# First causal attention: four heads of a group at once in three rounds instead of two heads in six, and the norms of a batch a group earlier

## The reference, cut to what matters

```python
attn = jnp.einsum('bhqd,bhkd->bhqk', q, k) * scale
attn0 = jnp.where(mask, 0.0, attn)
attn = conv_general_dilated(attn0, kernels, ...)   # 3x3 for each (batch, head)
attn = jnp.where(mask, -jnp.inf, attn)
p = jax.nn.softmax(attn, axis=-1)
out = jnp.einsum('bhqk,bhkd->bhqd', p, v)
return out @ proj_W + proj_b
```

## Time and profile before

| | us |
|---|---|
| three runs | 1775.22, 1777.56, 1786.68 |
| median | 1777.56 |
| the profiled execution | 1798.3, its span 1796.6 |
| of it the sixteen groups of the first attention (136.0 to 522.9) | 386.9 |

### The profile page before, as it was taken

The page is one execution under the profiler, slowest core; times in us unless marked ns, Lnnn a source line. Parts: engine busy times, 40 slices in busy tenths (PEclk is TensorE's granted clock), DMA queues, the critical chain, the costliest instruction groups (busy, mean ns, idle before and its releaser), DMA issues. The chain is left out here.

```text
span 1796.6 us, 26122 instructions
## 1 busy us (share of the span) xinstructions
PE 1290.6 (72%) x9324; PEld 773.9 (43%) x9324; DVE 1040.1 (58%) x2987; ACT 534.9 (30%) x1061; POOL 598.8 (33%) x744
## 2 busy tenths in 40 slices
PE   1378898998866893566454499789866988987820
PEld 0333344443434893465454388323325953332210
DVE  2455565565642344799999466435334435457797
ACT  0123343333322551222131133124313522323310
POOL 7032322224133253111032444101244531155675
PEclk9988997899987996555555599869857998867665
DMA  4900000000004121643351121310001220022232
GB/s 127 338 1 1 1 1 0 1 1 13 1 12 131 45 72 49 155 111 102 82 140 30 40 60 56 122 39 1 13 24 47 72 66 12 0 71 67 80 99 82
DMA packets 74246, 106.20 MB, mean 59 GB/s; under 512 B 11501, under 2 KB 55712, under 8 KB 71616
## 3 DMA queue, kind: packets, MB, share of 16 engines
q1 hardware_dynamic: 59968, 72.16, 14.3%
q0 software_dynamic: 14144, 32.32, 5.9%
HBM read 77.10 MB, written 27.33 MB: 58 GB/s over the span
## 5 line engine op out<-in xcount | busy, mean ns | idle before, releaser
L833 POOL DMA_INDIRECT y_d<-arena,goal x138 | 132.4, 960 | 185.8 <-DVE arena L916 112.0
L2032 POOL DMA_INDIRECT wide<-in_w_ud,arena x128 | 130.5, 1020 | 82.0 <-DVE arena L2063 45.1
L1701 DVE CUSTOM_DVE_ANT_0 arena<-ps,far 128x512 f32<-128x512 f32 (+3 forms) x256 | 117.8, 488 | 59.6 <-PE ps L1375 59.0
L2959 PE MATMUL ps<-wide,arena 78*128 78x32 bf16 x3840 | 110.1, 187 | 49.9 <-ACT wide L3072 41.5
L1290 POOL TENSOR_SCALAR_AFFINE_SELECT arena<-arena 128x260 f32<-128x260 f32 (+1 forms) x128 | 53.1, 427 | 255.8 <-ACT arena L1568 255.8
L2959 PEld LDWEIGHTS ps<-wide,arena 78*128 78x128 bf16 x3840 | 109.3, 104 | 56.2 <-ACT wide L3072 45.4
L1012 PEld LDWEIGHTS ps<-arena 128*128 128x128 f32 (+1 forms) x1012 | 123.2, 191 | 4.1
L1012 PE MATMUL ps<-arena 128*128 128x128 f32 (+1 forms) x1012 | 123.6, 274 | 0.0
L1568 ACT ACTIVATE arena<-ps 128x1024 f32<-128x1024 f32 (+1 forms) x96 | 84.6, 882 | 106.8 <-PE ps L1397 106.6
L1397 PE MATMUL ps<-arena 32*128 32x128 f32 (+3 forms) x512 | 112.2, 486 | 1.1 <-DVE arena L1720 1.1
L2583 DVE TENSOR_REDUCE arena<-ps 128x6 f32<-128x462 f32 (+1 forms) x96 | 55.2, 582 | 84.0 <-PE ps L2323 76.8
(11 more groups left out here) (514 smaller groups left out, 2637.7 us busy)
## 6 DMA issues: line engine op xcount, KB each, us to landing
arena<-low_d SPq DMA_DIRECT2D x32, 780.0 KB
xs_d<-zrow SPq DMA_DIRECT2D x1, 10320.0 KB, 35.6
arena<-xs_d SPq DMA_DIRECT2D x69, 129.0 KB, 2.1
arena<-y_d SPq DMA_DIRECT2D x16, 256.0 KB, 3.2
arena<-in_w SPq DMA_DIRECT2D x2, 1408.0 KB
y_d<-arena,goal POOLq DMA_INDIRECT x138
wide<-in_Wfc SPq DMA_DIRECT2D x1, 2048.0 KB, 11.5
wide<-in_Wproj SPq DMA_DIRECT2D x8, 256.0 KB, 6.2
```

The source lines that it names most:

```text
L833: pool.indirect_dma_start(out=y_d, in_=yb[:, i % 2, c, :], in_offset=None, out_offset=bass.IndirectOffsetOnAxis(ap=goal[:, i % 4, c:c + 1] ...
L1701: ins = nc.vector.tensor_tensor_reduce(junk[:, n % 2, 384 * i:384 * i + w], ps[:, n % 2, 384 * i:384 * i + w], far[:, T - w:T], 1.0, 3 * N ...
L2032: pool.indirect_dma_start(out=rows_g[t % 4][:, h, :], out_offset=None, in_=A["w_ud"], in_offset=bass.IndirectOffsetOnAxis(ap=eidi[:, t % 8 ...
L2959: mm = nc.tensor.matmul(ps[:, 2 * (i % 3) + h // 2, col:col + 4 * HD], ring[m_ % 4][:, h * NK + p_, t % 2 * P:t % 2 * P + P], table[n // 4 ...
```

## The change

Six rounds of two heads become three rounds of four heads, with the same key tiles in each round. The four heads' scores go to banks 2 to 5, one bank each, in every round, so the scores of a round wait for all exponentials of the round before. The exponentials stay 1024 wide: two instructions (two heads each) in the first and second round, one over four heads in the third. `pt` is one buffer for four heads, in which each round has its own columns. `select` works on four heads at once. The loops of TensorE and ScalarE are rewritten for three rounds; on GpSimd `products` now stands ahead of the last `select`, and `rstd0` with `near_weights` moves from groups 2 and 6 to groups 1 and 5. On VectorE `outputs(G-1)` moves from behind `maximum_out` to between the ninth and the tenth maximum, `norms` moves to the end of groups 0 and 4, and `normed` to the start of groups 2 and 6.

```diff
--- before.py
+++ after.py
@@ -1166,7 +1166,7 @@
         def first_causal():
             at[0] = 0
             q3 = carve(3, T); kpad = carve(2, T + 2); kc = carve(3, T)
-            pt = carve(2, 2, 1280); junk = carve(2, T)
+            pt = carve(4, 1280); junk = carve(2, T)
             xnp = carve(2, T + 3); xn0 = carve(NT, D)
             stat = carve(2, NT, 6); mean = carve(2, NT, 2); rst = carve(2, NT)
             nq = carve(7, D); prod = carve(9, D); near_dots = carve(9, H); near_two = carve(2, 9, H)
@@ -1247,6 +1247,7 @@
 
             mean_uses = [(r0 + r, ts) for r0 in (0, 2) for ts in ((3,), (2, 0), (1,)) for r in range(2)]
             ROUNDS = [((0, 0),), ((1, 0), (3, 384)), ((2, 0),)]
+            exps_after = lambda n: 5 * (n // 3) + (2, 4, 5)[n % 3]
             COL = {0: 0, 1: 512, 3: 896, 2: 1024}
 
             with nc.Block() as block:
@@ -1283,12 +1284,12 @@
                                                 pb0[:, :].unsqueeze(1).to_broadcast([P, NT, D]), ALU.add).then_inc(c["pb"], 1)
 
                     def select(n):
-                        pool.wait_ge(c["exp"], n + 1)
+                        pool.wait_ge(c["exp"], exps_after(n))
                         for kt, _ in ROUNDS[n % 3]:
                             w = min(T - P * kt, P + 2)
-                            v = pt[:, n // 3 % 2, :, COL[kt]:COL[kt] + w]
+                            v = pt[:, :, COL[kt]:COL[kt] + w]
                             ins = nc.gpsimd.affine_select(out=v, in_=v, compare_op=ALU.is_ge, fill=0.0, base=-2,
-                                                          pattern=[[0, 2], [1, w]], channel_multiplier=-1)
+                                                          pattern=[[0, 4], [1, w]], channel_multiplier=-1)
                         ins.then_inc(c["sel"], 1)
 
                     rstd0(0)
@@ -1303,21 +1304,19 @@
                     for G in range(G4):
                         nb, nt = near_key(G)
                         to_experts = lambda t: scatter(pool, 0, G // 4 - 2, rows0, twins0, t, t + 1) if G % 4 == 3 and G >= 11 else None
-                        for rd in range(3):
-                            select(6 * G + rd)
+                        select(3 * G)
                         to_experts(0)
-                        if G % 4 == 2 and G // 4 + 2 < B:
+                        if G % 4 == 1 and G // 4 + 2 < B:
                             rstd0(G // 4 + 2)
                             near_weights(G // 4 + 2)
-                        select(6 * G + 3)
+                        select(3 * G + 1)
                         to_experts(1)
                         if G % 4 == 2 and G >= 6:
                             R_.rstd_of(pool, ch, G // 4 - 1)
-                        select(6 * G + 4)
-                        to_experts(2)
                         if nb < B:
                             products(nb, nt)
-                        select(6 * G + 5)
+                        to_experts(2)
+                        select(3 * G + 2)
                         to_experts(3)
                         if G % 4 == 2 and G // 4 + 2 < B:
                             residual_bias(G // 4 + 2)
@@ -1384,30 +1383,28 @@
                         mm.then_inc(turn7, 1)
 
                     def scores(G, rd):
-                        n = 6 * G + rd
+                        n = 3 * G + rd
                         if rd == 0:
                             pe.wait_ge(free7_dve, emptied(place7["mz", G])[1])
                             pe.wait_ge(c["kc"], G + 1)
-                        if n >= 2:
-                            pe.wait_ge(c["exp"], n - 1)
-                        for kt, o in ROUNDS[rd % 3]:
-                            for i in range(2):
-                                r = rd // 3 * 2 + i
+                        if n:
+                            pe.wait_ge(c["exp"], exps_after(n - 1))
+                        for kt, o in ROUNDS[rd]:
+                            for r in range(4):
                                 rows = slice(32 * r, 32 * r + 32)
-                                mm = nc.tensor.matmul(ps[:, 2 + n % 2 * 2 + i, o:o + T - P * kt], kc[rows, G % 3, P * kt:P * kt + P],
+                                mm = nc.tensor.matmul(ps[:, 2 + r, o:o + T - P * kt], kc[rows, G % 3, P * kt:P * kt + P],
                                                  q3[rows, G % 3, P * kt:T], start=True, stop=True)
                         mm.then_inc(c["s"], 1)
 
                     def weighted(n):
-                        G, rd = n // 6, n % 6
+                        G, rd = n // 3, n % 3
                         pe.wait_ge(c["sel"], n + 1)
                         if rd == 0 and G:
                             pe.wait_ge(c["pvout"], G)
-                        for kt, _ in ROUNDS[rd % 3]:
-                            for i in range(2):
-                                r = rd // 3 * 2 + i
+                        for kt, _ in ROUNDS[rd]:
+                            for r in range(4):
                                 mm = nc.tensor.matmul(ps[32 * r:32 * r + HD + 1, 6, P * kt:T], v9[:, G // 4 % 3, kt, 4 * (G % 4) + r, :],
-                                                      pt[:, n // 3 % 2, i, COL[kt]:COL[kt] + T - P * kt], start=kt == 0, stop=kt == 2)
+                                                      pt[:, r, COL[kt]:COL[kt] + T - P * kt], start=kt == 0, stop=kt == 2)
                         mm.then_inc(c["pv"], 1)
 
                     def outputs_turned(G):
@@ -1454,40 +1451,34 @@
                         scores(G, 0)
                         top(2)
                         if G:
-                            weighted(6 * G - 1)
-
+                            weighted(3 * G - 1)
                         top(3)
-                        scores(G, 1)
-                        top(4)
                         if G + 2 <= last:
                             keys(G + 2)
+                        top(4)
                         top(5)
-                        weighted(6 * G)
+
+                        scores(G, 1)
                         if G % 4 == 1 and G >= 5:
                             joined(G // 4 - 1)
-
                         top(6)
-                        scores(G, 2)
-                        top(7)
                         if nb < B:
                             shifted(nb, nt, 0)
+                        top(7)
+                        weighted(3 * G)
                         top(8)
-                        weighted(6 * G + 1)
-
-                        top(9)
-                        scores(G, 3)
-                        top(10)
                         if G:
                             outputs_turned(G - 1)
-                        top(11)
-                        weighted(6 * G + 2)
+                        top(9)
+
+                        scores(G, 2)
                         if nb < B:
                             shifted(nb, nt, 1)
-
-                        scores(G, 4)
+                        top(10)
+                        weighted(3 * G + 1)
+                        top(11)
                         if nb < B:
                             shifted(nb, nt, 2)
-                        weighted(6 * G + 3)
                         if G % 4 == 1 and G >= 5:
                             projected(G // 4 - 1)
                         if G % 4 == 2 and G // 4 + 2 < B:
@@ -1498,12 +1489,9 @@
                             R_.logits(pe, take, G // 4 - 2)
                         if G % 4 == 2 and G >= 10:
                             R_.places(pe, take, G // 4 - 2)
-
-                        scores(G, 5)
-                        weighted(6 * G + 4)
                         if G + 1 <= last:
                             maximum_rows(G + 1)
-                    weighted(6 * last + 5)
+                    weighted(3 * last + 2)
                     outputs_turned(last)
                     R_.logits(pe, take, 2)
                     joined(B - 1)
@@ -1560,16 +1548,17 @@
                         ins.then_inc(free7_act, 1)
 
                     def exps(G, rd):
-                        n = 6 * G + rd
+                        n = 3 * G + rd
                         act.wait_ge(c["s"], n + 1)
-                        if n >= 6:
-                            act.wait_ge(c["pv"], 3 * (n // 3 - 2) + 3)
-                        o, w = ((0, 512), (512, 512), (1024, 256))[rd % 3]
-                        nc.scalar.activation(pt[:, n // 3 % 2, :, o:o + w], ps[:, 2 + n % 2 * 2:4 + n % 2 * 2, 0:w], ACT.Exp, scale=SCALE)\
-                            .then_inc(c["exp"], 1)
+                        if G:
+                            act.wait_ge(c["pv"], n - 2)
+                        o, w, heads = ((0, 512, 2), (512, 512, 2), (1024, 256, 4))[rd]
+                        for r in range(0, 4, heads):
+                            nc.scalar.activation(pt[:, r:r + heads, o:o + w], ps[:, 2 + r:2 + r + heads, 0:w], ACT.Exp, scale=SCALE)\
+                                .then_inc(c["exp"], 1)
 
```

(34 more changed lines are left out.)

## The result

The median went from 1782.12 us (four runs of the kernel before in the same session) to 1731.16 us (1724.08 to 1734.80). The ratio is 0.971, interval 0.965 to 0.977. The forecast was 1746, with a range of 1712 to 1787.

A forecast was written before the change was run, and what follows sets the result against it. TensorE was taken to set the pace, with VectorE in chains it waits for. The groups fall from 386.9 to 328.5 us at full clock, 58 gained, less 27 for the clock, rounded 32: 1777.6 - 32 = 1746 us, range 1712 to 1787.

The forecast's parts named there:

- The mechanism: TensorE, plain group: four heads cost what two do, saving 2.4 us on weighted values and 1.5 on scores; 20.54 to 16.6.
- The rival in which four column groups don't run side by side: Weighted values: 2.4 us x 16 = 39 us come back, giving 1785 us; chance 0.13.
- the one in which the clock falls twice a group: Pauses at the third maximum product and before `maximum_rows`: 28 falls cost 95 us against 58 gained, 1815 us; chance 0.08.
- the rival of the exponentials: One set of score banks makes TensorE wait in two rounds per group, a microsecond a group lost, 1762 us; chance 0.14.
- The rival in which the clock stays up: Pauses pull TensorE's clock down no more than once or twice; 58 us gained, 1720 us; chance 0.20.
- The clock term: Groups 1 to 10: pauses over 2 us make TensorE's clock fall eight times, 3.4 us each, 27 us lost.
- The sum at full clock: All sixteen groups at 2.4 GHz: 328.5 us against 386.9 before, 58 us gained; plain group 19.3 us.
- The chain from the last shifted product to the third maximum product: Groups 0 to 10: copy, `products`, `near_scores`, first maximum take 7.0 us; TensorE has 4.7 beside it, so 2.3 sticks out.
- the extras of groups 1 to 10: Norms and picks, join, `projected` with `maximum_rows`: 24 us on top of ten plain groups, 193 + 24 = 217.
- The join: VectorE, groups 4 and 8: 4.9 us, of which the chain covers 1.7, so 3.2 us in each.
- The moves: Earlier `outputs(G-1)` and moved norms remove waits of 0.92, 1.68 and 2.72 us, inside the 19.3; moved work costs 2.4 per batch.
- The exponentials: ScalarE ahead of the next round's scores: margin 0.6 us in groups 11 to 13, 1.9 in the others; no cost.

The follow-up runs named there:

- run with halves apart: Changed kernel with the weighted values issued two heads at a time again, a maximum product between the pairs: 1763.61 us, ratio 0.986.
- run with scores apart: Changed kernel with scores issued two heads at a time again in the first and third round: 1786.37 us, ratio 0.999.
- the late near scores: Changed kernel with `near_scores` of a group done in the next group, behind `mixed_keys`, six maxima later: 1785.18 us, ratio 1.002.
- the spread-out join: Changed kernel with the eight instructions of `join` between the maxima of groups 5, 9 and 13, its transposes later: 1743.98 us, ratio 0.978.
- four fills: Changed kernel with 22 products nobody reads ahead of the queries in groups 0, 5, 9 and 13: 1753.90 us, ratio 0.986.
- one maximum later: Changed kernel with `near_scores` of a group behind the first maximum of the next group instead of ahead of it: 1730.48 us, ratio 0.975.

## Why the prediction was right, and which terms were off

**The mechanism** was right in its main step: TensorE's work per plain group falls by 4 us (predicted 20.54 to 16.6, measured 16.55), of it 2.4 for the weighted values, which the run with halves apart confirms. The rival in which four column groups don't run side by side is refuted, and so is the one in which the clock falls twice a group: it lost 31 us in the stage, not 95. So is the rival of the exponentials: TensorE waits for them 1.1 us in all in front of L1395. The rival in which the clock stays up fails too, though its time, 1720, is nearer to the result than mine. The stage was to give 31 us (58 less 27) and gave 49.8. The terms, measured for each group as in the table above:

| | predicted | measured |
|---|---|---|
| groups 1 to 10 at full clock | 217 | 201.7 |
| groups 11 to 13 at full clock | 55.5 | 55.6 |
| groups 0, 14, 15 at full clock | 56.0 | 49.1 |
| lost to the clock | 27 | 30.7 |
| stage | 355.5 | 337.1 |

**The clock term** had the right size, but partly by luck. I took eight falls of 3.4 us in groups 1 to 10. There products lost 13.2 us, as falls in groups 5 and 8 lay over pauses (group 8: 2.9 us at 1.2 GHz, nothing lost). The other 17.5 us were lost in groups 0, 11, 12, 13 and 15, where I had put none. That is most of why group 11 takes 22.6 us where I wrote 18, and half of why group 12 takes 23.6 where I wrote 16; the other half is the wait of 5.00 us behind the join. That groups 11 to 13 agree with my sum at full clock, 55.6 against 55.5, is luck: one by one they take some 19, 20 and 17 us, where I had 18, 16 and 21.5.

**The sum at full clock is the step that failed**, 22 us too high. Ten of them are the plain group: 19.3 us predicted, 18.35 measured. The chain from the last shifted product to the third maximum product is as predicted, 6.9 us (216.38 to 223.30) against 7.0. The idle time in it was predicted as one pause of 2.3 us; it is 1.78 in three pieces, 0.62, 0.40 and 0.76. The term mis-sized is the rest of the group, TensorE's work from the third maximum product on: 18.35 - 6.9 = 11.4 us, where I had 12.1. Its work in a group is as predicted, but more of it ran beside the chain: 6.92 - 1.78 = 5.1 us, where I had 4.7. On top of that I had rounded the group up by 0.2. Some six more are the extras of groups 1 to 10, 24 us predicted and 201.7 - 10 x 18.35 = 18 measured. The last seven are group 0, which takes 21.0 us at full clock where I had 25.4 (it is idle for 6 us and not for 11; the 11 was a misreading, as group 0 of the kernel before has 21.45 us of work in 28.19 and so is idle for 6.7), and group 15 with 15.0, where I had let the scatters keep it at 17.6.

**The join**, among those extras, was too cheap. I took 4.9 us, of which 3.2 stick out. It takes 6.5 (235.10 to 241.62), as it now runs beside GpSimd, and the wait is 5.92 us with a fall of the clock that doubles the queries. That is group 5's 29.5 us. In group 8 the pause behind the join cost 5, and the one in group 12, where nothing ran on GpSimd, is 5.00 us with a join of 4.8.

**The moves** I had inside the group's sum. Alone, on the kernel before, they give 11 us. Taking the norms' move back from the changed kernel costs 10 to 21.

**The exponentials** I priced at nothing with 0.6 to 1.9 us of margin. It held, but the timeline and the run with scores apart show that the margin is smaller, 1.2 us in group 4 and next to nothing in eight others; this term was right by less than I wrote.

What stays open is what lets the clock fall at one pause and not at the next. A wait of 0.92 us did and didn't, one of 1.55 did, and edits elsewhere moved the longest low stretch from group 6 to group 1, or lengthened the one in group 5. The runs show where it lands and what it costs there; they don't show why there. The split of work and clock is worked out from the profiles and not made by a run that holds the clock.

## What to carry to other kernels

Small products on separate row and column groups of TensorE were worth packing four wide, and the gain could be priced from the row of two. When a schedule that looks better is slower, part TensorE's lost time at the low clock from the rest before you call the schedule worse: here two edits that shortened a visible wait, the late near scores and the spread-out join, made the kernel slower through the clock, and a low stretch of 10.2 us cost 2.8 us over a pause and 5 over dense work. Look up in each group where a pause stands before you fill it: two of four fills here stood behind theirs and cost 14 us. Try another engine's work at two or three places in the gaps, as six maxima later cost 56 us and one maximum later nothing.

## What the hardware showed that I had not expected

VectorE's `tensor_tensor` over 128x512 in fp32 takes 0.69 us alone and 1.64 and 1.01 us while GpSimd works on tensors in SBUF: L1725 at 237.48 under the products that run from 235.22 and the select behind them, L1726 at 239.16 under that select, against L1727 at 240.20, all of one shape. The same instructions in group 12 of the same kernel, where GpSimd does nothing from 412.75 on, take 0.69 us each:

```profile
415.18 0.69 DVE L1725 TENSOR_TENSOR arena<-arena 128x512 f32<-128x512 f32 x1
415.90 0.69 DVE L1726 TENSOR_TENSOR arena<-arena 128x512 f32<-128x512 f32 x1
```

The cost is uneven: L1724, under the same products, takes 0.80 us, only 0.11 more than in group 12. GpSimd's products take 3.36 us there and 2.96 without such company. The Trainium skill (SBUF — State Buffer, SBUF: two separate sides) says that a VectorE operation with two SBUF inputs and a GpSimd operation that reads SBUF exclude each other on a shared pair of ports for a whole instruction. The direction agrees with the rows; nothing here shows the lock itself, and L1724 was held up by 0.11 us only.

The select over twice the width costs 1.5 times as much, 656 ns against 427, so four heads in one instruction saved GpSimd time as well (groups by line, kernel after: count, busy us, mean ns, idle before):

```profile
L1291 POOL TENSOR_SCALAR_AFFINE_SELECT arena<-arena 128x520 f32<-128x520 f32 (+1 forms) x64 | 41.2, 656 | 162.7 <-ACT arena L1557 162.7
```

For the four column groups the surcharge over two was 0.09 us (1.06 against 0.97). The Trainium skill's factor for four row tiles (TensorE: Matmul & The Clock Gate, Part 3: Packing small matmuls) had led to an estimate of 0.3 us; the measurement decides for the smaller value here.
